# Linear attention and routing on one core: the state's share of the sums moved behind the scores, in tiles of 32x64

## The reference

```python
mod = (silu(c) @ wmod)                      # sa, ca, ga, sb, cb, gb for each sequence
h = layernorm(x) * (1 + ca) + sa
q, k, v = phi(h @ Wq), phi(h @ Wk), h @ Wv  # phi(x) = elu(x) + 1
S, z = S + k_t v_t^T, z + k_t               # scan over tokens, for each head
o_t = (S^T q_t) / max(z . q_t, 1e-6)
x = x + ga * (o @ Wo)
h = layernorm(x) * (1 + cb) + sb
# softmax over 8 logits, two best, position within the expert's 1,280 places
x = x + gb * sum_e combine_e * (silu(h @ Wg) @ Wd[e])
```

## Time and profile before

| | us |
|---|---|
| median of 3 runs | 843.34 (842.8 to 853.23) |
| profiled execution, its time | 848.72 |
| its span, first to last instruction | 847.0 |
| granted TensorE clock, mean | 0.966 |
| TensorE matmuls busy | 788.7 |
| VectorE, ScalarE, GpSimd busy | 577.3, 478.8, 484.0 |

### The profile page before, as it was taken

One profiled execution on the slowest core, in us unless ns is written; L12 is line 12 of the kernel. 1 busy time (PEld: TensorE's weight loads), 2 busy tenths in 40 slices (PEclk: granted clock), 3 DMA queues, 4 the chain that ended last, 5 costly groups with the idle time before them and its releaser, 6 DMA issues.

```text
span 847.0 us, 30958 instructions
## 1 busy us (share of the span) xinstructions
PE 788.7 (93%) x12583; PEld 688.8 (81%) x12583; DVE 577.3 (68%) x1869; ACT 478.8 (57%) x941; POOL 484.0 (57%) x621
## 2 busy tenths in 40 slices
PE   6899899999999999999999998878999997999994
PEld 4687778877877877877877876678999997999993
DVE  4577487878777877877877777522766646767762
ACT  4566467666667667667667664233554553554541
POOL 2203154656666776675766655462765746666764
PEclk9999799999999999999999999759999998999997
DMA  7409823142344132231021121014676655677653
GB/s 282 167 4 337 244 78 115 53 140 77 115 144 136 55 138 90 76 119 68 36 81 54 49 75 39 18 51 150 127 162 147 137 129 112 145 158 158 121 96 38
DMA packets 66844, 95.76 MB, mean 113 GB/s; under 512 B 7682, under 2 KB 48642, under 8 KB 66584
## 3 DMA queue, kind: packets, MB, share of 16 engines
q1 hardware_dynamic: 34136, 50.26, 18.9%
q0 software_dynamic: 21760, 31.66, 16.7%
q10 hardware_dynamic: 10816, 11.96, 4.5%
HBM read 38.97 MB, written 63.36 MB: 121 GB/s over the span
## 4 chain that ended last, share of the span: by engine, by line
PE 77%; DVE 9%; issue 5%; POOL 4%; DMA 3%; ACT 1%; POOLq 0%; SPq 0%; DVEq 0%; ACTq 0%
PE SCW L1727 12%; PE SCW L1398 8%; PE SB L1472 7%; PE SCW L1742 6%; PE SCW L1412 5%; PE PM L1501 5%; PE PJ L1501 3%; PE PM L1445 3%; PE SCW L1368 3%; PE SB L1742 3%; PE PM L1742 3%; PE PJ L1511 3%; PE PM L1460 3%; PE PM L1380 2%; PE PM L1511 2%
## 5 line engine op out<-in xcount | busy, mean ns | idle before, releaser
L514 POOL DMA_INDIRECT slot_rows<-Hrow,sloti x128 | 131.6, 1028 | 102.9 <-PE SCW L1412 60.2
L632 POOL DMA_INDIRECT out<-EX,desti x80 | 125.3, 1566 | 24.2 <-POOL idle L460 11.3
L460 POOL TENSOR_TENSOR idle<-mhalf 128x1 f32<-128x1 f32 x136 | 60.2, 443 | 76.3 <-DVE EX L1298 46.7
L994 DVE TENSOR_TENSOR Sm<-SCW,tri 128x512 f32<-128x512 f32 x128 | 82.1, 682 | 25.7 <-PE SCW L1368 23.9
L851 ACT ACTIVATE OTs<-SCW 128x512 f32<-128x512 f32 x64 | 38.3, 598 | 84.4 <-PE SCW L1412 84.4
L1398 PEld LDWEIGHTS SCW<-QT,Sbd 64*128 64x128 f32 x1024 | 65.3, 192 | 18.7 <-issue 18.0
L564 POOL TENSOR_TENSOR hT<-Sm,hT 128x512 fp32r<-128x512 f32 x30 | 38.3, 1278 | 67.4 <-ACT hT L686 66.6
L1398 PE MATMUL SCW<-QT,Sbd 64*128 64x64 f32 x1024 | 73.8, 284 | 3.0 <-DVE Sm L994 2.8
L701 ACT ACTIVATE N<-X,nb,rs 128x256 f32<-128x256 f32 x128 | 66.3, 592 | 7.5 <-POOL nb L574 4.8
L892 ACT ACTIVATE VA<-SCW 128x512 f32<-128x512 f32 x80 | 47.9, 598 | 38.5 <-PE SCW L1727 35.3
L1742 PE MATMUL SCW<-w_qkv,QS 128*128 128x256 f32 x416 | 62.9, 287 | 4.4 <-DVE QS L1270 4.4
(11 more groups left out here) (253 smaller groups left out, 2025.8 us busy)
## 6 DMA issues: line engine op xcount, KB each, us to landing
Hrow<-slot_rows SPq DMA_DIRECT2D x32, 516.0 KB, 4.4
slot_rows<-erow ACTq DMA_DIRECT2D x1, 10400.0 KB, 41.5
X<-x SPq DMA_DIRECT2D x16, 512.0 KB, 4.8
out<-X SPq DMA_DIRECT2D x16, 512.0 KB, 3.2
QT<-slot_rows SPq DMA_DIRECT2D x8, 516.0 KB, 3.8
Hrow<-MB SPq DMA_DIRECT2D x8, 512.0 KB, 3.5
MB<-mod_rows SPq DMA_DIRECT2D x1, 2048.0 KB
slot_rows<-Hrow,sloti POOLq DMA_INDIRECT x128
```

The lines of the kernel that those rows point to most:

```text
L460: pool.tensor_tensor(idle[:, k:k + 1], mhalf[:, 0:1], mhalf[:, 0:1], ALU.add).then_inc(breath, 1)
L514: pool.indirect_dma_start(xe, bass.IndirectOffsetOnAxis(sloti[:, par, k, t:t + 1], 0), Hrow[:, par, t, :], None, bounds_check=last_slot, o ...
L632: pool.indirect_dma_start(out, bass.IndirectOffsetOnAxis(desti[s % 2][:, a:a + 1], 0), Ys[s % 2][:, a, :], None, bounds_check=TOK - 1, oob ...
L994: dve.tensor_tensor(Smh(T % 2)[:, 2 * b:2 * b + 2], SCW[:, 2 * b:2 * b + 2, 0:2 * P].rearrange("p r (m i) -> p r m i", i=CH), tri64[:].uns ...
```

## The change

Nine edits, and the order of some work:

1. `OB` moves to columns 256 to 383 of the banks, and `from_state` right behind `scores`, without a wait for `sm_done`; `from_tile` waits for it instead. `sc_full` comes behind `from_state`. Between its two halves TensorE waits for its own scores (`scores_run`); the first half has each row group write the bank of its scores, the second half the neighbour's.
2. The state holds two heads for each 32 rows: stationaries of 32 rows and 64 columns in `from_state` (16 matmuls instead of 8), of 64 rows and 32 columns in `add_to_state` (16 of 34 moving columns instead of 8 of 68). `Sbd` and `Snew` are half as wide.
3. Two of the six parts of the second projection go ahead of `head_rows`.
4. `ln_tail` of the second norm moves from the end of n%4 = 0 to behind the masked scores of n%4 = 1.
5. In "place" only 6 of 9 steps are done in the slot, none of them inside `normalise_heads`; the other three follow behind the masked scores of the next slot.
6. ScalarE copies the logits ahead of the first of the next group's transposed halves.
7. Both halves of `modulation`, and the gates, move to `early(4)`; VectorE's masks go from `early(0)` to `early(2)`.
8. `e12` is filled first, and the first slots no longer wait for all constants.
9. SP loads row groups 4 to 7 behind the gates' broadcast.

```diff
-        OB = SCW[:, :, 0:DC * CH].rearrange("p (k b) (c i) -> p k b c i", k=2, c=DC)
+        OB = SCW[:, :, 2 * P:2 * P + DC * CH].rearrange("p (b k) (c i) -> p k b c i", k=2, c=DC)
...
+AHEAD = 2
+PLACED = 6
...
-            for g in range(2, EARLY):
+            for g in range(2, 4):
                 load_rows_of(g)
             sp.wait_ge(gate_fix, 5)
...
+            for g in range(4, EARLY):
+                load_rows_of(g)
...
-                if stage1 and q == 0:
-                    stage1_transposed(G, 0)
                 if routed and step == "columns":
                     logits_kept(g)
                 if stage1 and q == 0:
+                    stage1_transposed(G, 0)
                     stage1_hi(G, 0)
...
-                        if step == "place" and k < 9:
+                        if step == "place" and k < (9 if n >= TILES - 3 else PLACED):
...
+                if q == 1 and group_ok(gn - 1):
+                    dve.wait_ge(bn2, 4 * gn)
+                    ln_tail(st2, mv2, vp2, nm2, ag2, vpe2, gn)
+                if step == "columns" and group_ok(g - 1):
+                    for k in range(PLACED, 9):
+                        place(g - 1, k)
...
+                    if step == "place":
+                        normalise_heads(T, lambda: None, lambda: None)
+                    else:
+                        normalise_heads(T, between, between)
...
             def early(j):
                 if j == 4:
                     modulation(0)
-                if j == 6:
                     modulation(1)
...
-                last.then_inc(sc_full, 1)
+                last.then_inc(scores_run, 1)
...
-                for k in range(2):
-                    pe.wait_ge(sm_done, 2 * T + k + 1)
+                for other in range(2):
+                    if other:
+                        pe.wait_ge(scores_run, T + 1)
                     for cc in range(DC):
-                        for b in range(2):
-                            mm(OB[:, k, b, cc, :], Sbd[part(b), (2 * T + k) % 4, cc, :],
-                               QT[part(b), gp, cc, q * P + CH * k:q * P + CH * k + CH], start=(cc == 0), stop=False,
-                               skip_group_check=True)
+                        for r in range(4):
+                            rows, half = slice(32 * r, 32 * r + 32), slice(64 * (r % 2), 64 * (r % 2) + 64)
+                            k = (r + other) % 2
+                            last = mm(OB[half, k, r // 2, cc, :],
+                                      Sbd[rows, (2 * T + k) % 4, cc, :, :].rearrange("p s w -> p (s w)"),
+                                      QT[rows, gp, cc, q * P + CH * k:q * P + CH * k + CH], start=(cc == 0), stop=False,
+                                      skip_group_check=True)
+                last.then_inc(sc_full, 1)
 
             def from_tile(T):
 
                 q, gp = T % 4, (T // 4) % 2
                 if q % 2 == 0:
                     pe.wait_ge(pj_read, 6 * (T // 4) + 5 + q // 2)
+                pe.wait_ge(sm_done, 2 * T + 2)
...
             def add_to_state(n, g, routed, step):
+                            h = head(cc, r, 0)
+                            last = mm(PM[32 * r:32 * r + 32, k, cc * 2 * SW:(cc + 1) * 2 * SW],
+                                      Kn[part(k), cc * P + 32 * r:cc * P + 32 * r + 32],
+                                      VA[part(k), gp, q, h:h + 2, :].rearrange("p s w -> p (s w)"),
...
-                if tile_ok(n) and n > 0:
-                    scores(n)
+                if tile_ok(n):
+                    if n > 0:
+                        scores(n)
+                    from_state(n)
...
-                if tile_ok(n):
-                    from_state(n)
...
+                def second_projection(part):
+                    if q == 1:
+                        stage1_qk(G, 1, part)
+                    elif q == 2:
+                        stage1_qk(G, 3, part)
+                    elif q == 3:
+                        stage1_v(G, 1, part)
+
+                if stage1:
+                    if q > 0 and n >= -1:
+                        pe.wait_ge(state_read, n + 2)
+                    if q == 1 and group_ok(gn - 2):
+                        pe.wait_ge(taken, G - 2 + 1)
+                    second_projection(slice(0, AHEAD))
                 if tile_ok(n):
                     head_rows(n)
-                if stage1 and q > 0 and n >= -1:
-                    pe.wait_ge(state_read, n + 2)
                 if stage1:
-                    if q == 1:
-                        if group_ok(gn - 2):
-                            pe.wait_ge(taken, G - 2 + 1)
-                        stage1_qk(G, 1)
-                    elif q == 2:
-                        stage1_qk(G, 3)
-                    elif q == 3:
-                        stage1_v(G, 1)
+                    second_projection(slice(AHEAD, 6))
```

98 lines of the change are left out of this document (45 added, 53 removed).

## The result

The changed kernel takes 839.65 us, median of 20 runs (834.5 to 848.76); the kernel before took 845.04 in 20 runs beside it (837.54 to 853.23). The ratio is 0.9946, with an interval of 0.9923 to 0.997. The forecast was 804 us, 790 to 829: of the 40 us that it took off, about 5 came. The profiled execution took 840.02 us, its span is 838.2 us, its granted clock 0.963. The forecast took 40.3 off a span of 847.0, which makes 806.7, so 31.5 us of the span are to be explained.

A forecast was written before the change was run, and what follows sets the result against it. It took the order of TensorE's work to be the time. Slots -25.4 and +2.1, waits and a slow first block -13.0, start -4: together -40.3 us from a median of 843.3, predicting 804 us, range 790 to 829.

The forecast's parts named there:

- from_state: Moved behind the scores in small tiles: next projection +0.49 us, 1.03 us saved ahead of add_to_state, net -0.54 us a slot.
- B: Rival: from_state's tiles in alternating column halves run one after another, +25 us, 829 us; chance 0.10.
- D: Rival: a floor of 25 ns for each of the 64 new instructions, 837 us; chance 0.05.
- E: Rival: slower, a floor of 33 ns an instruction as if small tiles never overlapped, 870 us; chance 0.03.
- add_to_state and from_tile: The state sum as 32 smaller instructions instead of 16: no change taken, bounds 0.27 to 0.8 us.
- The masked scores move: Masked copy ends near 2.5 us, from_tile needs it at 3.5; POOL's send_row shifts 0.35 us, VectorE's saving priced at nothing.
- T%4 = 1: Slot of 8.50 us: the waits for An and Sm both go, TensorE gains 0.54 + 0.44 = 0.98 us.
- T%4 = 3: Slot of 7.79 us, counted among 47 slots that each gain 0.54 us, together -25.4 us.
- T%4 = 0: add_to_state waits for the h2T copies: each slot loses 0.15 us, 14 slots +2.1 us; only the An wait is won.
- Start: Both modulations ahead of the first projection: +1.9 - 1.9 - 2.5 - 1.7 (clock), about -4 us, bounds 0 and -5.
- F, instruction supply: Rival: a TensorE stop as in tile 8, with its low clock 7 us, comes twice or never: 796 or 812; chance 0.05.
- C, new waits: Rival: VectorE or ScalarE late for from_tile or the evictions, 0.3 us in each slot, 823 us; chance 0.11.

The follow-up runs named there:

- wide: The kernel before with only the move: OB in its own columns, old-tile from_state right behind the scores after a self-wait; 890.45 us, ratio 1.0445.
- paced: The changed kernel with two of POOL's row sends (T%4 = 0 and 2) put behind av_done; 833.08 us, ratio 0.9859 to the kernel before.
- after: The changed kernel itself, first measurement and trace; 839.65 us, ratio 0.9946 to the kernel before.
- after2: The changed kernel run once more, nothing altered; 837.28 us, ratio 0.9911 to the kernel before.
- noinit_a: The changed kernel without the 10.4 MB write that marks all expert places empty; 861.87 us, ratio 1.0083 to the kernel before.
- noinit_b: The kernel before without the 10.4 MB write that marks all expert places empty; 846.57 us, ratio 0.9869 to the kernel before.
- after3: The changed kernel run again in a later series, nothing altered; 840.32 us, ratio 0.991 to the kernel before.
- best1: The changed kernel with two POOL sends behind av_done and from_tile ahead of add_to_state in T%4 = 3; 832.78 us, ratio 0.9818 to before.
- clear: The changed kernel with two sends behind av_done, from_tile ahead of add_to_state in T%4 = 3, no 10.4 MB write; 828.86 us, 0.9722 of before.
- onewait: The changed kernel without from_tile's second, redundant wait for the values; 871.73 us, ratio 1.0208 to the kernel before.

## Why the prediction failed, step by step

**The wait table, and what bounds the kernel.** Right that the order of TensorE's work is the time; wrong that what is cut from it comes back. A table of few waits says that covers suffice, not by how much. The prediction worked out the cover of `add_to_state` in T%4 = 0 only.

**from_state.** Right in the mechanism. L1387 comes 1.21 us behind the scores against 1.12, 0.09 too late in each slot; the self-wait is 0.2 us in wide against 0.12. The 32 instructions of L1408 hold the engine 0.72 us from start to start. Their row is 0.79 us long, above the 0.3 to 0.55 that were to show them: it begins at 0.49, while the scores' row still runs. Rivals B, D and E did not occur, as their L1380 would come at 1.5 us or later.

**add_to_state and from_tile: "no change".** `add_to_state` holds the engine 0.21 to 0.26 us (0.40 before), better than said. `from_tile` was the loss that the sum put at nothing: by the medians it holds the engine 1.24 us in T%4 = 0 and 0.93 in T%4 = 2, against 0.77 and 0.76 before, which is 8.3 us over 13 groups. (The prediction's last sentence names a slower `from_tile` as a sign of failure, behind more instructions and not under the sends.)

**The masked scores move, POOL's send_row "shifts by 0.35 and has av_done ahead of it anyway".** This step failed. It asked whether a send comes too late, not on what it falls. In T%4 = 0 the first send used to lie under `from_state` (260.51 in before, 2.15 us behind the scores, with `from_tile` at 262.01); now it comes 4.06 us behind the scores and lies under `from_tile`. In T%4 = 2 the move of `from_state` brings the third send there, as wide shows. `Sm` itself was in time, as predicted.

**T%4 = 1.** -1.27 us against -0.98. Right in kind, and a little more than said.

**T%4 = 3, inside "47 slots at -0.54".** The step that failed in the sum. The 1.03 us of `from_state` had hidden the eviction of the first value projection. The slot is 0.16 longer instead of 0.54 shorter: 0.70 x 13 = 9.1 us. The same question that found `h2T` would have found it: what does `add_to_state` wait for in each of the four kinds of slot.

**T%4 = 0.** The `h2T` wait is as worked out (0.88 us, 14 times); without the collision the slot is 7.44 to 7.70 in 8 of 14 groups of paced, against 7.5; in the others the heads are late, or a stop lies in it.

**Start.** Scores(0) come at 27.05 us (27.5 predicted), 3.1 us earlier than before. The term of 1.7 us for the clock failed: the full clock behind scores(0) did not come. The stretch of the earlier trace rows, 31.0 to 34.5 us, does show 0.93 in after, but the half clock has only moved ahead with the scores.

```profile
26.66 0.36 PE L1458 MATMUL PM<-VA,AK 64*32 64x34 f32 x32 [1.81 <-issue]
27.05 0.70 PE L1375 MATMUL SCW<-QM,KT 32*64 32x128 f32 x32
```

```profile
28.10:31.50 3.40, 3.40 (x44) 3.06 (x43) 0.11 (x1) 1.02 (x2) 0.00 (x0) 0.50 0.97 354
```

The projection behind scores(0) takes 2.52 us in after and 2.53 in before, from its start to that of the next row. The 2.48 us in which TensorE waited for `mod12` are gone, but `add_to_state` ahead of the scores now waits 1.81 us. after2 has that wait too (1.78 us) and no stretch at half clock behind it, so the clock can stay up there.

**F, instruction supply.** Named with 0.05 and "twice or not at all"; it came four times. Up to tile 12, 14.4 us are missing. Of these, 3 x 1.14 = 3.4 are the slots' losses above, 6.7 the three stops more (8.9 against 2.2), and about 3.4 the clock: the stretches at 0.50 behind the four stops are 17.1 us long, which costs up to 8.5, where before's one of 10.2 us costs 5.1. The start was to gain 4 and gained 3.1, another 0.9. Together that is 14.4. That it comes out so closely is luck, as the next figures show. Without the write noinit_a's tile 12 leads noinit_b's by 6.4 us, where 11.1 was forecast. The count differs between executions (tile 12 at 134.3, 129.0 and 131.1 in after, after2, after3), so this share is good to some 5 us. By its own 7.2 us the rival would give 797 or 811, not 796 or 812.

**C, new waits.** It was near in size (it said 0.3 us a slot, and the two waits are 20.8 us in 61 slots) and wrong in place: ScalarE's evictions, at `add_to_state`, not `Sm` at `from_tile`. Its condition should have been worked out for each kind of slot rather than given one chance.

**What stays open.** The waits, the collisions and the stops are each seen in the traces and taken away by a run. How much time each returns is not: best1 takes away the wait of T%4 = 3 and its total stays, and clear, with the eviction covered, two sends moved and no write, gains 17.7 us over noinit_b and not 40. Part of what is left there is `An`, late again in T%4 = 0 (3.4 us in five waits of clear, 222 to 505 us).

## What to carry to other kernels

When work is moved forward in an engine's order, list for every kind of slot what the instruction behind the gap waits for and how long ago that was ready: the moved work was a cover for all of them. Then shift every other engine's timeline by the same amount and see what falls on what; runs of very small matmuls and a GpSimd that issues indirect DMAs must be kept apart. Last, when a stretch at a low clock is to go, look for it anew from the event that it follows, and not at its old time. That more instructions cost more while a large transfer is under way fits the traces, but no run tested it alone.

## What the runs showed of the hardware

- 64 instructions of 64x17 by 64 columns take 0.62 to 0.66 us (median) from first to last start when GpSimd issues nothing, and 0.93 us on average when an indirect DMA lies over more than 0.2 us of them (26 tiles of after). In the 855 series it is 1.76 us (30 tiles of onewait), where one send of 1.06 us costs more than its own length. A send that ends within the first 0.12 us costs nothing in 11 of 12 tiles (T%4 = 1 in after, 0.64 to 0.68 us). By what path the two engines meet is not shown.
- The kernels' level, 846 or 855 us for before, differs between series, and the cost of the collision with it (5 to 8 us of gaps against 30). What sets it is open. The ratio of changed to unchanged kernel changes its sign with it: 0.99 for after at 846, 1.02 for onewait at 855.
- In the 855 series the granted clock fell to 0.50 for 3.4 us at a time in tiles whose `from_tile` had stood still under a send (nine of 13 tiles with T%4 = 0 in onewait). In before there is none in such a tile.
- While a 10.4 MB write is under way, some instruction fetches of 16 KB come with stops of TensorE of 2 to 2.8 us and a granted clock of 0.50 behind them. The stops end 1.2 to 1.5 us behind the fetch. With eight pieces instead of one there are still such stops; without the write there are none of over 1.5 us in its time. A few like them come elsewhere, near 34 or 38 us and in tile 40.
